# Cross attention on one core: scores in groups of three items, values in turns of one and two key tiles

## The reference, cut to what matters

```python
xq  = ada_ln(x, cond, Wss_q, bss_q)            # x:   1 x 4096 x 512, float32
xkv = ada_ln(ctx, cond, Wss_kv, bss_kv)        # ctx: 1 x 3202 x 512
q = (xq @ Wq + bq).reshape(B, 4096, 16, 32)
k, v = split(xkv @ Wkv + bkv)                  # 16 heads of 32
scores = einsum('bqhd,bkhd->bhqk', q, k) / sqrt(32)
attn = softmax(scores, axis=-1)
out = einsum('bhqk,bkhd->bqhd', attn, v)
return x + (out.reshape(B, 4096, 512) @ Wp + bp)
```

## Time and profile before

| | |
|---|---|
| median of 3 runs | 2374.38 us (2374.38 to 2377.04) |
| span of the profiled execution | 2371.8 us |
| what lies around the span, against the median | 2.6 us |
| attention, first to last exponential | 257.1 to 2326.5 us |
| a middle unit | 64.07 us |
| TensorE, DVE, ACT busy | 97%, 82%, 76% |

### The profile page before, as it was taken

The page is one execution under the profiler, slowest core; times in us unless marked ns, Lnnn a source line. Parts: engine busy times, 40 slices in busy tenths (PEclk is TensorE's granted clock), DMA queues, the critical chain, the costliest instruction groups (busy, mean ns, idle before and its releaser), DMA issues.

```text
span 2371.8 us, 34855 instructions
## 1 busy us (share of the span) xinstructions
PE 2308.8 (97%) x12234; PEld 1028.5 (43%) x12234; DVE 1936.1 (82%) x1153; ACT 1806.9 (76%) x1822; POOL 62.2 (3%) x46
## 2 busy tenths in 40 slices
PE   7998799999999999999998999999999999999998
PEld 3456344444443444444443444444443334444343
DVE  4564588888889888888887888898888988888886
ACT  1333588888888888888887888888888977777772
POOL 1111000000001000000001000000001000000000
PEclk9999799999999999999999999999999999999999
DMA  6777911111117211111137111111154222332223
GB/s 231 265 267 259 185 54 54 54 53 53 52 27 147 65 54 54 54 44 54 53 72 158 54 54 35 35 47 53 53 114 92 68 60 67 95 94 78 72 60 127
DMA packets 135663, 211.65 MB, mean 89 GB/s; under 512 B 15016, under 2 KB 48296, under 8 KB 135532
## 3 DMA queue, kind: packets, MB, share of 16 engines
q1 hardware_dynamic: 124572, 186.70, 29.1%
q0 software_dynamic: 3376, 12.85, 1.7%
q10 hardware_dynamic: 7584, 10.49, 1.2%
HBM read 138.18 MB, written 71.82 MB: 89 GB/s over the span
## 4 chain that ended last, share of the span: by engine, by line
PE 85%; issue 1%; POOL 1%; ACT 1%; DVE 1%; DMA 0%; SPq 0%; ACTq 0%; POOLq 0%; DVEq 0%
PE ring L890 33%; PE o_ps L905 32%; PE l_ps L964 4%; PE l_ps L973 4%; PE l_ps L985 4%; PE l_ps L926 1%; POOL g_max L859 1%; PE ring L985 1%; PE o_ps L911 1%; PE l_ps L923 1%; PE ring L878 1%; ACT pt L1126 1%; DMA vg<-v_full 0%; DVE acc L1202 0%; DVE s_max L1213 0%
## 5 line engine op out<-in xcount | busy, mean ns | idle before, releaser
L1126 ACT ACTIVATE pt<-ring,shift 128x1024 f32<-128x1024 f32 x1600 | 1678.5, 1120 | 312.5 <-PE ring L890 296.4
L1202 DVE TENSOR_TENSOR acc<-acc,pt 128x2048 f32<-128x2048 f32 x672 | 1516.7, 2288 | 104.4 <-ACT pt L1126 104.0
L890 PE MATMUL ring<-qs,ks 128*128 128x512 f32 x3200 | 1005.2, 436 | 18.9 <-ACT pt L1126 18.9
L905 PE MATMUL o_ps<-pt,vg 128*32 128x512 f32 x6400 | 855.6, 607 | 0.0
L890 PEld LDWEIGHTS ring<-qs,ks 128*128 128x128 f32 x3200 | 563.2, 189 | 470.8 <-ACT pt L1126 306.2
L1202 DVE TENSOR_TENSOR acc<-pt 128x2048 f32<-128x2048 f32 x64 | 146.7, 2292 | 140.6 <-ACT pt L1126 140.6
L905 PEld LDWEIGHTS o_ps<-pt,vg 128*32 128x32 f32 x6400 | 126.2, 108 | 294.7 <-issue 225.7
L973 PEld LDWEIGHTS l_ps<-work 128*128 128x128 f32 x672 | 86.0, 190 | 121.6 <-issue 121.6
L964 PE MATMUL l_ps<-work 128*128 128x256 f32 x336 | 117.4, 431 | 0.0
L973 PE MATMUL l_ps<-work 128*128 128x128 f32 x672 | 114.0, 297 | 0.0
L331 PE MATMUL bank<-xt,wq 128*128 128x512 f32 x256 | 111.9, 595 | 0.0
(11 more groups left out here) (79 smaller groups left out, 670.1 us busy)
## 6 DMA issues: line engine op xcount, KB each, us to landing
qs<-q_split SPq DMA_DIRECT2D x128, 256.0 KB, 5.0
ks<-k_split SPq DMA_DIRECT2D x80, 320.0 KB, 6.6
work<-ctx_t SPq DMA_DIRECT2D x21, 1024.0 KB, 7.6
k_split<-work SPq DMA_DIRECT2D x42, 256.0 KB, 2.1
x_bias<-xb ACTq DMA_DIRECT2D x8, 1024.0 KB, 9.1
q_split<-hi SPq DMA_DIRECT2D x8, 1024.0 KB, 9.2
q_split<-lo SPq DMA_DIRECT2D x8, 1024.0 KB, 11.2
o_sums<-o_sb SPq DMA_DIRECT2D x32, 256.0 KB, 7.4
```

Of the source, the lines that this page charges most:

```text
L890: mm = nc.tensor.matmul(ring[:, bank + i, :], ks[:, h, t * P:(t + 1) * P], qs[U.par][:, h, :], start=True, stop=not exact)
L905: mm = nc.tensor.matmul(o_ps[cols, :], vg[:, t, cols], pt[t % PR][:, h, :], start=(t == 0), stop=False, skip_group_check=True)
L1126: nc.scalar.activation(pt[t % PR][:, 2 * pair:2 * pair + 2, :], ring[:, bank:bank + 2, :], ACT.Exp, scale=SCALE, bias=bias[:, :]).then_inc ...
L1202: nc.vector.tensor_tensor(a[:, :, :], (pt[t - 1] if k <= 2 else a)[:, :, :], pt[t % PR][:, :, :], ALU.add).then_inc(p_added, 1)
```

## The change

The loop over tiles becomes a loop over 17 groups k of three items. Group k scores items 3k + 3 to 3k + 5, six matmuls in a row (those past item 50 are the next unit's first three), and then weighs every tile whose two items are among 0 to 3k + 2: one tile for even k, two tiles for odd k. `side(t)` still follows the values of tile t. The pairs are tiles (1, 2), (4, 5), (7, 8) and so on to (22, 23); the single tiles are 0, 3, 6, and so on to 24. The next unit's third item now stands ahead of the values of tile 24. The ring, the buffers, the waits inside `scores` and `weigh`, and the programs of ACT, DVE, POOL and the DMA queues are the same.

```diff
 def unit(U, nxt, side):
-    for t in range(NT):
-        for n in (2 * t + RING, 2 * t + RING + 1):
+    t = 0
+    for k in range(ITEMS // RING):
+        for n in range(RING * (k + 1), RING * (k + 2)):
             if n < ITEMS:
                 scores(U, n, exact)
             elif nxt is not None:
                 scores(nxt, n - ITEMS, False)
-        weigh(U, t)
-        if t == NT - 1:
-            weigh_tail(U)
-        side(t)
-    if nxt is not None:
-        scores(nxt, RING - 1, False)
+        while t < NT and 2 * t + 1 < RING * (k + 1):
+            weigh(U, t)
+            if t == NT - 1:
+                weigh_tail(U)
+            side(t)
+            t += 1
```

## The result

The changed kernel took 2427.64 us (median of 4 runs, 2424.02 to 2428.67), the kernel before beside it 2374.38 (4 runs). The ratio is 1.0218, with a 95% interval of 1.0204 to 1.0233. I had forecast 2426 and a range of 2402 to 2446.

What follows compares the result with a forecast made beforehand. TensorE's order and starts were taken as the bound. Waits less saved weight changes gave +41.4 us in middle units and 52 us in all; span 2371.8 + 52, with 2.6 around it, made 2426 us, range 2402 to 2446.

Steps and rivals of the forecast that it cites:

- The bound: Whole kernel: TensorE's order and starts set the time; ACT and DVE have about 9 us to spare a unit.
- What is saved: Pairs without full-array side work after their first tile: 0.29 us each for score/value weight changes, 121 pairs, 35 us at most.
- The closed loop: Score, three exponentials, score: a pair's third item after a short group without side work waits 0.31 us.
- cold start: After a wait, first weights were not loaded under the matmul before: 0.11 us more, 0.42 in total with the wait.
- ACT's jobs: Middle unit, waits: copy of value sums 0.48 us, copy of denominators at pair (7, 8) 0.90, key split at pair (16, 17) 0.97.
- The middle unit: Waits 3.19 us, saved 0.87: +2.3 us each, +41.4 us over 18 units.
- The other units: Units outside the 18 middle ones: +2.6, +2.7, +1.3, +1.4 and +2.6 us.
- The 2.6 us around the span: Time outside the profiled span, added to 2371.8 + 52 us to reach 2426 us.
- The full gain: Exponentials start earlier or ACT runs ahead, no wait is left: -35 us, 2339 us; chance 0.04.
- copies and split hide: Only the regular waits remain in a middle unit, about 0 change, 2370 to 2380 us; chance 0.06.
- The clock did not fall: Judges the claim that TensorE's stops lower the granted clock once a unit: 54 us more, 2480 us; chance 0.06.

Runs made afterwards that it cites:

- shortened kernels: Kernel before and changed kernel, each with exponentials on 256 of the 512 queries: 2363.57 us and 2340.81 us.
- shortened grouped kernel: Changed kernel with every exponential on 256 of the 512 queries: 2340.81 us, ratio to before 0.9849.
- late copy: Changed kernel with ACT's copy of the value sums one exponential later, after item 2: 2407.53 us, ratio to before 1.0138.
- covered turns: Changed kernel with ACT's copies and key split later and side work on single tiles, five units in the old order: 2315.27 us, ratio to before 0.9737.
- three moves: Changed kernel with ACT's copy of the value sums, copy of the denominators and key split each made later: singly 2407.53, 2414.91, 2418.28 us; together 2388.5 us.
- same move of one copy: Copy of the value sums one exponential later: 2407.53 us on the changed kernel, 2400.78 us on the kernel before.
- l_copy_late: Changed kernel with ACT's copy of the denominators one tile later in groups 0 to 2: 2414.91 us, ratio to before 1.0176.

## Why the prediction was right

- **The bound.** TensorE set the pace before, and its order decided. Shown by the shortened kernels: halving the exponentials left a middle unit of before at 64.08 us.
- **What is saved.** 0.29 us a pair was too small; it is 0.35. Values of a pair stand 0.88 apart, not 0.91, and a further score item costs a little less than 0.465. With 121 pairs the most that could be gained is 42 us and not 35. A middle unit gives back 1.04 us, not 0.87.
- **The closed loop and its cold start.** Shown at the expected items. In units without side work, short group to pair and back took 3.02 + 0.88 + 2.56 = 6.46 us for three tiles (6.52 forecast, 6.39 before).
- **ACT's jobs.** Shown one by one: 0.46, 0.49 and 0.43 us a middle unit, where 0.48, 0.48 and 0.55 were worked out.
- **The middle unit.** +2.2 us against +2.3: 39.2 of the 54.9 us against 41.4. The waits in it are then 2.18 + 1.04 = 3.22 us, 3.19 forecast. They can also be read one by one, by the starts of the same items in the shortened grouped kernel, where the middle unit has no wait: the second unit of group 1 falls behind it by 0.43 us at item 5, 0.42 at item 8, 0.43 at item 14, 0.92 at items 19 and 20, and 1.02 at items 37 and 38 (forecast 0.48, 0.42, 0.42, 0.90, 0.97).
- **The other units.** The sum is near, its parts less so. Forecast and measured: first units of groups 2.6 and 4.7; last ones 2.7 and 2.0; first unit of the last group 0 and 2.4; its last six 2.6 and 0; the end after the last exponential 0 and 3.8. I had no term for the end. In the first units of groups I had said that the copy makes no wait behind the new shift; it does (item 5 starts 3.67 us after the first exponential, and 3.18 with the late copy). Part of the 4.7, 2.4 and 3.8 is a clock that stayed low for longer, below, for which I had no term either. The 2.6 us around the span were another mix: 1.6 us in the profiled execution of the changed kernel (2428.28 against 2426.7), and the rest came from setting the profiled execution of before against the median. Errors of both signs cancelled, and that the total came out 2 us off is partly luck.
- **The rivals.** The full gain needs a kernel in which no score waits; the groups were faster only with short exponentials or covered turns. That copies and split hide is refuted by the three moves. The clock did not fall in middle units: 1.00 in the one shown, with seven items of it on the list, and the clock record of the trace has no low stretch in any middle unit. What the Trainium skill's "TensorE: Matmul & The Clock Gate", A second HAM failure mode: psum-queue depth-cycling, says of short idles between groups of matmuls did not bear out here at waits under 0.5 us.

Of the last six units, five took 0.2 us more each (70.92 against 70.70; +0.4 forecast), and the very last, which ends here with the tail's exponential, 1.2 less.

The longer end has two parts. The last output step follows the values of tile 22, and these now stand behind the scores of the tail. The changed kernel, at its end:

```profile
2375.66 1.09 PE L878 MATMUL ring<-qs,kt 128*128 128x512 f32 x4
...
2377.67 1.13 PE L988 MATMUL l_ps<-work 128*128 128x512 f32 x2
...
2384.38 8.15 PE L988 MATMUL ring<-work 128*128 128x512 f32 x12 [2.68 <-DVE work L1241]
```

DVE adds that step's result, then makes a reciprocal, one addition of its own and the division for which TensorE waits (2.68 us here, 1.27 before). From this step to the matmuls behind the division it takes 6.71 us in both kernels, but the step starts 0.18 us after the last exponential's start and not 2.65 before it: 2.8 us, of which 1.2 are those by which the last unit is shorter. The other 1.0 us is the clock, below. In the shortened grouped kernel the same way takes 6.71 us too.

## What to carry to other kernels

Busy share tells which engine is the bound on average; whether a new order can use another engine's slack is decided in the shortest stretch between two waits, so write the loop down (score, so many exponentials, score) and compare it with the engine's own pace there. A ring that is filled in one go has no slack left in it: put other work of the bound engine in the short turns, and keep the consumer's small jobs out of the stretch that the bound engine waits for. And a small job's best place depends on the producer's order: the same move of one copy gave 20 us in one kernel and cost 26 in the other.

## What the runs showed of the hardware

A wait inside a run of matmuls costs more than its length. From the matmul that waited to the next one it takes 0.34 us and not 0.23: at 1050.84 above, its weight load starts together with it and not under the matmul before. Item 8 shows both parts in the middle unit: 0.32 us of wait and 0.10 more by the start of the next item.

The granted clock was low for longer at some starts of groups. In the changed kernel, at the start of group 1:

```profile
782.20:789.10 6.90, 6.43 (x17) 3.03 (x18) 2.29 (x1) 5.59 (x7) 0.00 (x0) 0.51 1.11 233
```

0.51 over 6.9 us, where before it was 3.4 us. TensorE stood 1.17, 0.27 and 0.27 us before three score items there:

```profile
781.39 0.74 PE L890 MATMUL ring<-qs,ks 128*128 128x512 f32 x2 [1.17 <-ACT pt L1129]
782.40 1.22 PE L890 MATMUL ring<-qs,ks 128*128 128x512 f32 x2 [0.27 <-ACT pt L1129]
783.89 1.22 PE L890 MATMUL ring<-qs,ks 128*128 128x512 f32 x2 [0.27 <-ACT pt L1129]
785.04 1.94 PE L905 MATMUL o_ps<-pt,vg 128*32 128x512 f32 x8
```

The lower level is 1.2 GHz; eight value matmuls take 1.94 us at it and 1.06 at 2.4 GHz. The same 6.8 us stand in the clock record at the start of the last group and after the last exponential, where it was 3.4 before; at the start of group 2 it is 10.2 us in both kernels.

What this costs can be read from `l_copy_late`. Its program is that of the changed kernel in the last group and behind it, but its record has 3.4 us of low clock at each of the two places and not 6.8. The first unit of the last group runs alike up to item 6 and takes 58.32 us in all and not 59.64, and from the last exponential it takes 48.1 us and not 49.2. So 3.4 us more at the lower level cost 1.3 and 1.1 us, and some 1.3 of the 2.4 and 1.0 of the 3.8 us are this. For the 4.7 us of the two first units of groups 1 and 2 no such pair of runs exists. Why it is 3.4 us in one execution and 6.8 in another is open. The four runs of the changed kernel have mean clocks of 0.983 to 0.985, and the shortest has the highest.
